# A CIN layer kernel: paired 64-row tiles for the Gram products, x1 stored with d innermost, and its sum over d moved to GpSimd

## The chip, the cores and the metric

The kernel runs on one core of a Trainium2 chip. The metric is the device time of one execution in microseconds. The profile's names for the engines are PE for TensorE (PEld for its weight loads), DVE for VectorE, ACT for ScalarE, POOL for GpSimd and SP for the engine that issues most DMAs.

## The reference, cut to what matters

Thirty-nine embedding tables are gathered into `e` of shape (512, 39, 16), a three layer CIN is applied with sums over `d` as its outputs, and a small MLP follows.

```python
def _cin_layer(X0, Xi, W, b):          # B, F0, D = 512, 39, 16; H = 128 outputs in each layer
    Wr = W.reshape(H, F0_, Fi)
    return jnp.einsum('hjk,bjd,bkd->bhd', Wr, X0, Xi) + b[None, :, None]
...
for W, b in Ws:                        # three layers
    Xi = _cin_layer(X0, Xi, W, b)
    res.append(Xi.sum(axis=2))         # the sum over d
z = jnp.concatenate(res, axis=1)
...
h = jnp.concatenate([z, dense_ctx], axis=1)
h = jnp.maximum(h @ W_top1 + b_top1, 0.0)
h = jnp.maximum(h @ W_top2 + b_top2, 0.0)
y = h @ W_top3
```

## The kernel before

The 512 samples are cut into 16 chunks of 32 samples, so a chunk has 32 x 16 = 512 columns (sample, d). A chunk is cut again into 4 groups of 8 samples, 128 columns (8 samples x 16 values of d), which are the 128 rows of a layer-1 product.

- **Layer 0** of the next chunk is built while the current one is in layer 1. GpSimd forms seven products `prod0` from shifted copies of x0 (`multiply0`), ScalarE rounds them to a high half (`round_product`), GpSimd subtracts for the low half (`split_product`), and TensorE adds three fp32r matmuls for each of the seven into the bank `acc0`. They stand behind the blocks of `L0_AFTER`, the last behind (3, 1), which means block 1 of group 3.
- **x1** is `acc0` plus a bias. ScalarE writes it to SBUF as `x1` (L759), copies that to the rounded `x1h` (L762), and VectorE writes the rest as `x1l` (L674).
- **Layer 1** of a group is 10 blocks of four fields each. A block is three matmuls of 512 columns (L528, L529, L530). Blocks marked A in `OWNERS = "ADADAADADA"` go to the PSUM banks `ya` and ScalarE scales them into `prods` (L779, four instructions a block, three in the last one); blocks marked D go to the banks `yd` and VectorE runs them into a chain (L651). There are 4 banks `ya` and 2 banks `yd`; a block waits with its first weight load (L528) until ScalarE or VectorE has emptied its bank. Two reductions of VectorE (L666) give `x2t`, which is x2 of the group with its 128 columns on the partitions.
- **Layer 2** only needs its sum over d, so a **Gram product** is formed for each group: `x2t` (128 rows of sample and d) times `diag`, a 128 x (8 x 40) matrix that holds the row's own x0 in the columns of its own sample. `gram_group` (L511) is one fp32 matmul of 320 columns over all 128 rows; the trace shows each as two weight loads and two matmuls. It stands behind block `G_AFTER = 6` of the following group. GpSimd writes `diag` (L401), in two buffers, and ScalarE empties the bank `misc` into `gram` (L767).
- **Layout.** Gathered embeddings are transposed by two matmuls into `misc` (`lay_out`, L479 and L480), go to SBUF as `xt`, from there to DRAM (`store_x0`, L319), and come back as `x0` (`load_x0`, L328) for a second turn (`turn_x0`), which is two transposes, of 117 rows (L487) and of 39 rows (L488), since x0 holds three shifted copies of 39 fields. They also come back as the tiles of layer 0 (L294, L288).
- **The sum of x1 over d** goes to `z`. For chunks 0 to 14 VectorE does it with one reduction inside the next group of blocks (`sum_dims` at (2, 0), L680); for the last chunk GpSimd does it in four additions that halve the number of values each time (`sum_dims_last`, L410 and L414).

Each engine runs a list written by hand; what binds them are semaphores. The loops over the middle chunks are real loops on VectorE and ScalarE and unrolled on TensorE, GpSimd and SP.

## Time and profile before

| what | us |
|---|---|
| median of 3 runs (lowest, highest) | 654.07 (651.15, 656.03) |
| the profiled execution, its own time | 654.38 |
| its span in the trace | 652.5 |
| busy: PE, DVE, ACT, POOL | 617.7, 581.6, 558.5, 470.9 |

The span runs from the first to the last instruction of the core, and the execution's own time is 1.9 us longer. The granted clock of TensorE was 1.0 in the whole span, the 2.4 GHz level. In the trace, first work takes about 38 us, then the chunks follow each other, and the last 50 us are the second layer's sum and the MLP.

### The profile page before, as it was taken

What the parts mean: (1) busy time and instruction counts of PE and PEld (TensorE: products, weight loads), DVE (VectorE), ACT (ScalarE), POOL (GpSimd) and SP (SyncE); (2) the same over time, 40 slices, a digit from 0 to 9 for tenths busy, and PEclk for the clock granted to TensorE, in tenths of its full rate; (3) what the DMA queues carried; (4) which work ended last, traced back from release to release, by engine and by line L of the source; (5) the groups of instructions that cost most, each with busy time, mean ns of one, the idle gap of its engine ahead of it and who ended that gap; (6) DMA issues with size and microseconds to landing.
All of it is one profiled execution on the core that took longest, in us unless ns stands there. A gap on an engine that the chain in (4) does not pass through costs nothing.

```text
span 652.5 us, 14351 instructions
## 1 busy us (share of the span) xinstructions
PE 617.7 (95%) x2595; PEld 477.3 (73%) x2595; DVE 581.6 (89%) x1233; ACT 558.5 (86%) x1767; POOL 470.9 (72%) x442
## 2 busy tenths in 40 slices
PE   0389999999999999999999999999999999999998
PEld 0146788787878787878788787878787878876673
DVE  0549999999999999999999999999999999999980
ACT  3048899999999999999899989999999999999782
POOL 6778898979797989989798979798987656420000
DMA  7533404131222314040414132231405050000200
GB/s 228 135 78 88 125 19 126 34 105 53 79 81 49 109 21 137 9 137 17 126 32 121 39 91 67 67 91 39 120 8 149 1 150 5 12 18 1 65 1 0
DMA packets 44274, 46.16 MB, mean 71 GB/s; under 512 B 20896, under 2 KB 27264, under 8 KB 44233
## 3 DMA queue, kind: packets, MB, share of 16 engines
...
HBM read 44.30 MB, written 1.31 MB: 70 GB/s over the span
## 4 chain that ended last, share of the span: by engine, by line
PE 88%; issue 4%; DVE 4%; POOL 1%; ACT 1%; DMA 1%; DVEq 0%
PE ya L528 12%; PE ya L530 12%; PE ya L529 12%; PE yd L528 9%; PE yd L530 8%; PE yd L529 8%; PE misc L511 5%; PE acc L500 4%; PE acc L499 3%; PE acc L501 3%; PE acc L504 2%; DVE chain L651 2%; POOL emb L390 1%; PE yd L611 1%; PE yd L609 1%
## 5 line engine op out<-in xcount | busy, mean ns | idle before, releaser
L779 ACT ACTIVATE prods<-ya,x0t 128x128 f32<-128x128 f32 x1472 | 452.0, 519 | 40.8 <-PE ya L530 37.8
L651 DVE SCALAR_TENSOR_TENSOR chain<-yd,x0t,chain 128x128 f32<-128x128 f32 x768 | 218.2, 343 | 4.9 <-remote 4.0
L390 POOL DMA_INDIRECT emb<-in_tables,rows x160 | 158.4, 990 | 35.4 <-issue 24.3
L528 PE MATMUL ya<-w1h,x1h 128*128 128x512 f32 (+1 forms) x384 | 166.4, 433 | 3.2 <-ACT prods L779 2.1
L437 POOL TENSOR_TENSOR prod0l<-prod,prod0h 120x512 fp32r<-120x512 f32 x98 | 127.6, 1302 | 47.8 <-ACT prod0h L788 47.2
L529 PE MATMUL ya<-w1l,x1h 128*128 128x512 f32 (+1 forms) x384 | 147.5, 384 | 0.0
L530 PE MATMUL ya<-w1h,x1l 128*128 128x512 f32 (+1 forms) x384 | 147.2, 383 | 0.0
L305 POOL TENSOR_TENSOR prod<-tiles,x0a 120x512 f32<-120x512 f32 x105 | 137.3, 1308 | 12.5 <-issue 4.2
L666 DVE TENSOR_REDUCE x2t<-prods 128x128 f32<-128x1792 f32 x64 | 129.2, 2019 | 2.4 <-issue 0.3
L666 DVE TENSOR_REDUCE prods<-prods 128x128 f32<-128x1536 f32 x64 | 111.7, 1746 | 0.1
L528 PE MATMUL yd<-w1h,x1h 128*128 128x512 f32 x256 | 102.5, 400 | 1.9 <-DVE prods L651 1.6
L530 PE MATMUL yd<-w1h,x1l 128*128 128x512 f32 x256 | 100.6, 393 | 0.0
L529 PE MATMUL yd<-w1l,x1h 128*128 128x512 f32 x256 | 100.2, 391 | 0.0
L528 PEld LDWEIGHTS ya<-w1h,x1h 128*128 128x128 f32 x384 | 72.2, 188 | 20.3 <-issue 4.3
L529 PEld LDWEIGHTS ya<-w1l,x1h 128*128 128x128 f32 x384 | 72.4, 189 | 15.5 <-issue 0.7
L530 PEld LDWEIGHTS ya<-w1h,x1l 128*128 128x128 f32 x384 | 72.0, 188 | 13.7
L788 ACT ACTIVATE prod0h<-prod 120x512 fp32r<-120x512 f32 x98 | 67.5, 689 | 1.1 <-POOL prod L305 1.1
L528 PEld LDWEIGHTS yd<-w1h,x1h 128*128 128x128 f32 x256 | 48.1, 188 | 20.5 <-DVE prods L651 8.2
L401 POOL TENSOR_TENSOR diag<-x0t,const 128x320 f32<-128x320 f32 x64 | 46.6, 728 | 17.0 <-PE misc L511 16.7
L529 PEld LDWEIGHTS yd<-w1l,x1h 128*128 128x128 f32 x256 | 48.0, 188 | 10.9 <-issue 0.5
L530 PEld LDWEIGHTS yd<-w1h,x1l 128*128 128x128 f32 x256 | 48.1, 188 | 10.3
L651 DVE SCALAR_TENSOR_TENSOR prods<-yd,x0t,chain 128x128 f32<-128x128 f32 x128 | 47.3, 464 | 0.0
...
## 6 DMA issues: line engine op xcount, KB each, us to landing
...
emb<-in_tables,rows POOLq DMA_INDIRECT x160
...
```

Of the source, the lines that this page charges most:

```text
L305: engine.tensor_tensor(prod0[:, i % L0_PRODS, :], tiles[:, slot, :], x0a[:, :], ALU.mult).then_inc(prod0_ready, 1)
L390: pool.indirect_dma_start(emb[:, c % 2, fo * D:(fo + 1) * D], None, a["tables"], bass.IndirectOffsetOnAxis(ap=rows[:, c, fo:fo + 1].bitcas ...
L401: pool.tensor_tensor(diag[:, n % 2, :, :], row.to_broadcast([P, GB, F1]), mask.to_broadcast([P, GB, F1]), ALU.mult).then_inc(diag_ready, 1)
L437: pool.tensor_tensor(prod0l[:, k % L0_PRODS, :], prod0[:, i % L0_PRODS, :], prod0h[:, k % L0_PRODS, :].bitcast(F32), ALU.subtract).then_in ...
L511: pe.matmul(misc[:, 0:GB * F1], x2t[:, g % 2, :], diag[:, g % 2, :, :].rearrange("p b j -> p (b j)"), start=True, stop=True).then_inc(g_do ...
L528: pe.matmul(out, x1h[:, c % 2, xs], w1h[:, cols], start=True, stop=False)
L529: pe.matmul(out, x1h[:, c % 2, xs], w1l[:, cols], start=False, stop=False)
L530: pe.matmul(out, x1l[:, c % 2, xs], w1h[:, cols], start=False, stop=True).then_inc(ready, 1)
L651: dve.scalar_tensor_tensor(out, product, x, run if step else b1[:, :], ALU.mult, ALU.add).then_inc(yd_used, 1)
L666: dve.tensor_reduce(out, src, AX.X, ALU.add).then_inc(sums_done, 1)
L779: mm = act.activation(prods[:, :, slot_of(q) + i], ya[(NA * g + k) % YA][:, i * H:(i + 1) * H], ACT.Copy, scale=turned(c)[:, g * F1 + j:g ...
L788: act.activation(prod0h[:, k % L0_PRODS, :], prod0[:, i % L0_PRODS, :], ACT.Copy).then_inc(prod0_high, 1)
```

## The change

Four things change together.

1. **The Gram product in row tiles.** The order of the columns of a chunk is changed so that partitions 0 to 63 of a group hold one half of its samples and 64 to 127 the other. A group's Gram product becomes two matmuls of 64 rows and 160 columns, one on the upper 64 rows, one on the lower, into two PSUM banks (`pair`). Two groups are done at one place (`gram_groups`, L527 of the new kernel): four matmuls behind (0, 6) and four behind (2, 6), none behind (1, 6) and (3, 6) except in the last chunk. `pair` takes a second bank, so `ya` has 3 banks in place of 4. `diag` is 160 columns wide, in four buffers.
2. **Layout.** x0 is stored in halves: 64-byte pieces where there were 128-byte ones on the way to DRAM, and rows of two 1 KB pieces on the way back. x0 holds two shifted copies, and its turn is two transposes of 78 rows.
3. **x1 with d innermost.** ScalarE writes `x1` from `acc0` in another order, and writes `x1h` from `acc0` too, no longer from `x1`, with no wait between them.
4. **The sum over d** of every chunk is done by GpSimd in place, in four additions, after its third product (after the sixth in chunk 0). VectorE's reduction is gone.

```diff
@@ -36,12 +36,15 @@
 CHUNKS = B // CB
 GB = P // D
 GROUPS = CB // GB
+HB = GB // 2
+HROWS = P // 2
...
 FT = P // D
-XB = 3
+XB = 2
...
-YA, YD = 4, 2
+YA, YD = 3, 2
+DIAGS = 4
...
-SUM_DIMS, SPLIT_X1 = (2, 0), (3, 0)
+SUM_AFTER, SUM_AFTER_0 = 2, 5
+SPLIT_X1 = (3, 0)
...
-        diag = sb("diag", [P, 2, GB, F1])
+        diag = sb("diag", [P, DIAGS, HB, F1])
...
-        scratch = nc.dram_tensor("x0_rows", (CHUNKS, FP, COLS), F32, kind="Internal").ap()
-
...
+        acc0, pair = ps("acc0"), ps("pair", (P, 2, 512))
+        misc = pair[:, 0, :]
...
         def chunk_rows(c):
-            return scratch[bass.ds(c, 1), :, :].rearrange("c r n -> (c r) n")
+            return scratch[bass.ds(c, 1), :, :, :].rearrange("c h r n -> r (c h) n")
+
+        def in_halves(x):
+            return x.rearrange("p (h n) -> p h n", h=2)
...
-                engine.dma_start(x0a[u * R0:(u + 1) * R0, :], chunk_rows(x)[0:R0, :]).then_inc(x0a_in, 16)
+                engine.dma_start(in_halves(x0a[u * R0:(u + 1) * R0, :]), chunk_rows(x)[0:R0]).then_inc(x0a_in, 16)
...
-                engine.dma_start(tiles[a:b, i % L0_TILES, :],
-                                 chunk_rows(x)[row:row + b - a, :]).then_inc(tile_in[i % L0_TILES], 16)
+                engine.dma_start(in_halves(tiles[a:b, i % L0_TILES, :]),
+                                 chunk_rows(x)[row:row + b - a]).then_inc(tile_in[i % L0_TILES], 16)
...
-                by_row = chunk_rows(x).rearrange("(f o) n -> f (o n)", f=FI)
-                for i, cols in enumerate((slice(0, FT * COLS), slice(FT * COLS, FO * COLS))):
-                    sp.dma_start(by_row[:, cols].rearrange("f (p b) -> p f b", b=CB),
-                                 xt[0:(cols.stop - cols.start) // CB, i, :].rearrange("p (f b) -> p f b", f=FI),
+                by_row = scratch[x, :, :, :].rearrange("h (f o) n -> (h f) (o n)", f=FI)
+                for i, cols in enumerate((slice(0, FT * HCOLS), slice(FT * HCOLS, FO * HCOLS))):
+                    sp.dma_start(by_row[:, cols].rearrange("q (p b) -> p q b", b=CB // 2),
+                                 xt[0:(cols.stop - cols.start) // (CB // 2), i, :].rearrange("p (q b) -> p q b", b=CB // 2),
...
-                    sp.dma_start(x0[g * F:(g + 1) * F, 0:COLS - g], chunk_rows(x)[0:F, g:COLS]).then_inc(x0_in, 16)
+                    sp.dma_start(in_halves(x0[g * F:(g + 1) * F, :])[:, :, 0:HCOLS - g], chunk_rows(x)[0:F, :, g:HCOLS]).then_inc(x0_in, 16)
...
             def block_diagonal(c, g):
                 n = GROUPS * c + g
                 pool.wait_ge(x0t_ready, c + 1)
-                wait_done(pool, g_done, n - 1)
+                wait_done(pool, g_done, n - DIAGS + 1)
                 row = x0t[:, c % XT, g * F1:(g + 1) * F1].rearrange("p (o j) -> p o j", o=1)
-                mask = const[:, C_MASK:C_MASK + GB].rearrange("p (b o) -> p b o", o=1)
-                pool.tensor_tensor(diag[:, n % 2, :, :], row.to_broadcast([P, GB, F1]),
-                                   mask.to_broadcast([P, GB, F1]), ALU.mult).then_inc(diag_ready, 1)
-
-            def sum_dims_last():
-
-                pool.wait_ge(x1h_ready, CHUNKS)
-                terms, count = x1[:, :].rearrange("p (g d b) -> p g d b", g=GROUPS, d=D), D
+                mask = const[:, C_MASK:C_MASK + HB].rearrange("p (b o) -> p b o", o=1)
+                pool.tensor_tensor(diag[:, n % DIAGS, :, :], row.to_broadcast([P, HB, F1]),
+                                   mask.to_broadcast([P, HB, F1]), ALU.mult).then_inc(diag_ready, 1)
+
+            def sum_dims(c):
+
+                pool.wait_ge(x1_ready, c + 1)
+                if c == 0:
+                    pool.wait_ge(l0_done, T0 + z_tiles)
+                terms, count = x1[:, :].rearrange("p (q d) -> p q d", d=D), D
                 while count > 2:
                     count //= 2
-                    pool.tensor_tensor(terms[:, :, 0:count, :], terms[:, :, 0:count, :], terms[:, :, count:2 * count, :],
+                    pool.tensor_tensor(terms[:, :, 0:count], terms[:, :, 0:count], terms[:, :, count:2 * count],
                                        ALU.add).then_inc(z_adds, 1)
-                    pool.wait_ge(z_adds, {8: 1, 4: 2, 2: 3}[count])
-                out = z[:, (CHUNKS - 1) * CB:].rearrange("p (g b) -> p g b", g=GROUPS)
-                pool.tensor_tensor(out, terms[:, :, 0, :], terms[:, :, 1, :], ALU.add).then_inc(z_sums, 1)
+                    pool.wait_ge(z_adds, 3 * c + {8: 1, 4: 2, 2: 3}[count])
+                out = z[:, c * CB:(c + 1) * CB].rearrange("p (g h b) -> p h b g", g=GROUPS, h=2)
+                one, other = (terms[:, :, d:d + 1].rearrange("p (h b g) d -> p h b (g d)", h=2, g=GROUPS) for d in range(2))
+                pool.tensor_tensor(out, one, other, ALU.add).then_inc(z_sums, 1)
...
-                    if c == CHUNKS - 1 and i == 2:
-                        sum_dims_last()
+                    if i == (SUM_AFTER if c else SUM_AFTER_0):
+                        sum_dims(c)
...
                 pe.transpose(misc[:, 0:XB * F], by_group[:, 0, :], const[0:XB * F, C_ID:C_ID + XB * F])
-                pe.transpose(misc[:, XB * F:GROUPS * F], by_group[0:F, XB, :], const[0:F, C_ID:C_ID + F]
+                pe.transpose(misc[:, XB * F:2 * XB * F], by_group[:, XB, :], const[0:XB * F, C_ID:C_ID + XB * F]
...
-            def gram_group(n, g):
-                pe.wait_ge(sums_done, 2 * n + 2)
-                pe.wait_ge(diag_ready, n + 1)
-                wait_done(pe, g_ready, n)
-                pe.matmul(misc[:, 0:GB * F1], x2t[:, g % 2, :],
-                          diag[:, g % 2, :, :].rearrange("p b j -> p (b j)"),
-                          start=True, stop=True).then_inc(g_done, 1)
+            def gram_groups(ns):
+
+                pe.wait_ge(sums_done, 2 * ns[-1] + 2)
+                pe.wait_ge(diag_ready, ns[-1] + 1)
+                wait_done(pe, g_ready, ns[0])
+                for i, n in enumerate(ns):
+                    for h in range(2):
+                        half, cols = slice(h * HROWS, (h + 1) * HROWS), slice(i * HB * F1, (i + 1) * HB * F1)
+                        mm = pe.matmul(pair[:, h, cols], x2t[half, n % 2, :],
+                                       diag[half, n % DIAGS, :, :].rearrange("p b j -> p (b j)"), start=True, stop=True)
+                mm.then_inc(g_done, len(ns))
...
-                            wait_done(pe, g_ready, GROUPS * c + g - 1)
+                            wait_done(pe, g_ready, GROUPS * c)
...
                             pe.wait_ge(x0_ready, c + 3)
-                            wait_done(pe, g_ready, GROUPS * c + g - 1)
+                            wait_done(pe, g_ready, GROUPS * c + 2)
                             turn_x0(c + 2)
-                        if q == G_AFTER and (g or prev):
-                            if not prev and g == 1:
-                                pe.wait_ge(x0t_ready, 2)
-                            if lay and g == lay_after(prev)[0]:
+                        if q == G_AFTER and g == 0 and prev:
+                            pe.wait_ge(x0t_ready, min(c + 2, CHUNKS))
+                            gram_groups((GROUPS * c - 2, GROUPS * c - 1))
+                        if q == G_AFTER and g == 2:
+                            if lay:
                                 pe.wait_ge(x0_ready, c + 3)
-                            if lay and g == turn_after(prev)[0]:
-                                pe.wait_ge(x0t_ready, c + 3)
-                            gram_group(GROUPS * c + g - 1, (g - 1) % GROUPS)
+                            gram_groups((GROUPS * c, GROUPS * c + 1))
+                        if q == G_AFTER and g == 3 and c == CHUNKS - 1:
+                            gram_groups((GROUPS * c + 2,))
...
-                                if nxt and (g, half) == SUM_DIMS:
-                                    sum_dims(c)
                                 if nxt and (g, half) == SPLIT_X1:
...
-                act.activation(xt[0:FO * D - P, 1, :], misc[0:FO * D - P, P:2 * P], ACT.Copy).then_inc(x0_ready, 1)
+                def by_half(x, order):
+                    return x.rearrange(f"p ({order} b) -> p f h b", h=2, b=CB // 2)
+
+                act.activation(by_half(xt[:, 0, :], "h f"), by_half(misc[:, 0:P], "f h"), ACT.Copy)
+                act.activation(by_half(xt[0:FO * D - P, 1, :], "h f"), by_half(misc[0:FO * D - P, P:2 * P], "f h"),
...
-                act.activation(x1[:, :].rearrange("p (g n) -> p g n", g=GROUPS),
-                               acc0[:, :].rearrange("p (n g) -> p g n", g=GROUPS), ACT.Identity, bias=bias[:, 0:1]).then_inc(x1_ready, 1)
-                act.wait_ge(x1_ready, c + 1)
-                act.activation(x1h[:, bass.ds(c & 1, 1), :].rearrange("p c n -> p (c n)"), x1[:, :],
-                               ACT.Copy).then_inc(x1h_ready, 1)
-
-            def evacuate_gram(n):
+                act.activation(x1[:, :].rearrange("p (h q d) -> p h d q", h=2, d=D),
+                               acc0[:, :].rearrange("p (h d q) -> p h d q", h=2, d=D), ACT.Identity, bias=bias[:, 0:1]).then_inc(x1_ready, 1)
+                act.activation(x1h[:, bass.ds(c & 1, 1), :].rearrange("p c (g n) -> p (c g) n", g=GROUPS),
+                               acc0[:, :].rearrange("p (n g) -> p g n", g=GROUPS), ACT.Identity, bias=bias[:, 0:1]).then_inc(x1h_ready, 1)
+
+            def evacuate_gram(n, i=0):
                 act.wait_ge(g_done, n + 1)
-                act.activation(gram[:, :, bass.ds(n * GB, GB)],
-                               misc[:, 0:GB * F1].rearrange("p (b j) -> p j b", b=GB),
+                cols = slice(i * HB * F1, (i + 1) * HB * F1)
+                act.activation(gram[:, :, bass.ds(n * GB, GB)].rearrange("p j (h b) -> p j h b", h=2),
+                               pair[:, :, cols].rearrange("p h (b j) -> p j h b", b=HB),
                                ACT.Copy).then_inc(g_ready, 1)
 
...
-                        if q == G_AFTER + 1 and (g or prev):
-                            evacuate_gram(GROUPS * c + g - 1)
+                        if q == G_AFTER + 1 and (g == 2 or g == 0 and prev):
+                            evacuate_gram(GROUPS * c + g - 2, 0)
+                        if q == G_AFTER + 2 and (g == 2 or g == 0 and prev):
+                            evacuate_gram(GROUPS * c + g - 1, 1)
+                        if q == G_AFTER + 1 and g == 3 and not nxt:
+                            evacuate_gram(GROUPS * c + 2)
```

TensorE around block (2, 6) of a middle chunk, before. `misc` is the bank of the Gram product.

```order
L529 MATMUL yd0<-w1l,x1h 128x512
L530 MATMUL yd0<-w1h,x1l 128x512
L511 MATMUL misc<-diag,x2t 128x320
L528 MATMUL ya0<-w1h,x1h 128x512
L529 MATMUL ya0<-w1l,x1h 128x512
```

The same place after; L544 to L546 are the three matmuls of a block there.

```order
L545 MATMUL yd0<-w1l,x1h 128x512
L546 MATMUL yd0<-w1h,x1l 128x512
L527 MATMUL pair<-diag,x2t 128x160 x4
L544 MATMUL ya1<-w1h,x1h 128x512
L545 MATMUL ya1<-w1l,x1h 128x512
```

One matmul of 320 columns has become four of 160, and the banks `ya` are taken in another turn.

TensorE around block (3, 6) before, with blocks 5, 6 and 7 of the group.

```order
L530 MATMUL ya1<-w1h,x1l 128x512
L528 MATMUL yd0<-w1h,x1h 128x512
L529 MATMUL yd0<-w1l,x1h 128x512
L530 MATMUL yd0<-w1h,x1l 128x512
L511 MATMUL misc<-diag,x2t 128x320
L528 MATMUL ya2<-w1h,x1h 128x512
```

Blocks 7, 8 and 9 of group 3 after, in the same stretch of the program.

```order
L544 MATMUL ya1<-w1h,x1h 128x512
L545 MATMUL ya1<-w1l,x1h 128x512
L546 MATMUL ya1<-w1h,x1l 128x512
L544 MATMUL yd1<-w1h,x1h 128x512
L545 MATMUL yd1<-w1l,x1h 128x512
L546 MATMUL yd1<-w1h,x1l 128x512
L544 MATMUL ya2<-w1h,x1h 128x384
L545 MATMUL ya2<-w1l,x1h 128x384
```

The Gram product is gone from here, so nothing but blocks stands between the turn of x0 behind (3, 1) and block (0, 3) of the next chunk.

GpSimd from the second product of a chunk to the fourth, before.

```order
L305 TENSOR_TENSOR prod0<-tiles,x0a 120x512
L437 TENSOR_TENSOR prod0l<-prod0,prod0h 120x512
L401 TENSOR_TENSOR diag<-x0t,const 128x320
L390 DMA emb<-in_tables,rows 128x16
L305 TENSOR_TENSOR prod0<-tiles,x0a 120x512
L437 TENSOR_TENSOR prod0l<-prod0,prod0h 120x512
L390 DMA emb<-in_tables,rows 128x16
L305 TENSOR_TENSOR prod0<-tiles,x0a 120x512
```

The same stretch after; `w0_z` is the tensor whose end holds `z`.

```order
L314 TENSOR_TENSOR prod0<-tiles,x0a 120x512
L449 TENSOR_TENSOR prod0l<-prod0,prod0h 120x512
L410 TENSOR_TENSOR diag<-x0t,const 128x160
L399 DMA emb<-in_tables,rows 128x16
L314 TENSOR_TENSOR prod0<-tiles,x0a 120x512
L449 TENSOR_TENSOR prod0l<-prod0,prod0h 120x512
L421 TENSOR_TENSOR x1<-x1 128x32x8
L421 TENSOR_TENSOR x1<-x1 128x32x4
L421 TENSOR_TENSOR x1<-x1 128x32x2
L426 TENSOR_TENSOR w0_z<-x1 128x8x4
L399 DMA emb<-in_tables,rows 128x16
L314 TENSOR_TENSOR prod0<-tiles,x0a 120x512
```

The four additions stand ahead of a gather and of the fourth product, and `diag` is half as wide.

## Rows read from the trace of the kernel before

**Rows 1.** The page: busy time of the engines, and the chain that ended last.

```profile
PE 617.7 (95%) x2595; PEld 477.3 (73%) x2595; DVE 581.6 (89%) x1233; ACT 558.5 (86%) x1767; POOL 470.9 (72%) x442
...
PE 88%; issue 4%; DVE 4%; POOL 1%; ACT 1%; DMA 1%; DVEq 0%
```

**Rows 2.** Busy time by stretch: chunk 9, then the last; length, busy of PE, PEld, DVE, ACT, POOL, clock.

```profile
365.20:400.30 35.10, 35.09 (x154) 28.09 (x154) 33.87 (x75) 32.58 (x110) 30.47 (x29) 1.00 0.28 74
540.70:576.00 35.30, 34.50 (x151) 27.67 (x151) 34.45 (x79) 32.80 (x107) 15.83 (x20) 1.00 0.05 14
```

**Rows 3.** Waits in 365.2 to 505.6, four chunks: total, times, longest, us.

```profile
POOL prod0l L437 <- ACT prod0h L788: 11.8, 11, 2.0
...
PEld yd L528 <- DVE prods L651: 1.2, 3, 0.4
```

**Rows 4.** TensorE in order of time at a Gram product: start, length in us.

```profile
373.74 0.70 PE L511 MATMUL misc<-diag,x2t 128*128 128x320 f32 x2
...
374.51 0.40 PE L529 MATMUL ya<-w1l,x1h 128*128 128x512 f32 x1
```

**Rows 5.** The same view where the layout is transposed, behind (2, 1).

```profile
378.28 0.27 PE L479 MATMUL misc<-const,emb 128*128 128x128 f32 x1
378.38 0.27 PE L480 MATMUL misc<-const,emb 128*32 128x128 f32 x1
...
378.73 0.39 PE L529 MATMUL ya<-w1l,x1h 128*128 128x512 f32 x1
```

**Rows 6.** The same view where x0 is turned, behind (3, 1).

```profile
387.88 0.26 PE L487 MATMUL misc<-const,x 117*128 117x117 f32 x1
388.07 0.19 PEld L488 LDWEIGHTS misc<-const,x 39*128 39x128 f32 x1 [0.22 <-issue]
...
388.31 0.19 PEld L528 LDWEIGHTS ya<-w1h,x1h 128*128 128x128 f32 x1
...
388.42 0.19 PEld L529 LDWEIGHTS ya<-w1l,x1h 128*128 128x128 f32 x1
...
388.88 0.39 PE L530 MATMUL ya<-w1h,x1l 128*128 128x512 f32 x1
```

**Rows 7.** ScalarE in order of time from x1 to block (3, 5).

```profile
388.08 0.69 ACT L759 ACTIVATE x<-acc,bias 128x512 f32<-128x512 f32 x1
388.96 0.63 ACT L762 ACTIVATE x1h<-x 128x512 f32 x1 [0.19 <-issue]
390.25 1.31 ACT L779 ACTIVATE prods<-ya,x0t 128x128 f32<-128x128 f32 x4 [0.66 <-PE ya L530]
...
393.17 1.33 ACT L779 ACTIVATE prods<-ya,x0t 128x128 f32<-128x128 f32 x4
```

**Rows 8.** Weight loads in order of time: of block (0, 0), and of (0, 3).

```profile
394.12 0.19 PEld L528 LDWEIGHTS ya<-w1h,x1h 128*128 128x128 f32 x1
...
396.54 0.19 PEld L528 LDWEIGHTS yd<-w1h,x1h 128*128 128x128 f32 x1 [0.43 <-DVE prods L651]
```

**Rows 9.** Groups by line, every shape apart: count, busy, mean ns.

```profile
L401 POOL TENSOR_TENSOR diag<-x0t,const 128x320 f32<-128x320 f32 x64 | 46.6, 728 | 17.0 <-PE misc L511 16.7
...
...
L680 DVE TENSOR_REDUCE w_z<-x 128x512 f32 x14 | 16.0, 1144 | 0.0
```

**Rows 10.** GpSimd in order of time: a late product at 321.64, the last chunk's additions.

```profile
321.64 1.28 POOL L305 TENSOR_TENSOR prod<-tiles,x0a 120x512 f32<-120x512 f32 x1 [1.75 <-issue]
...
568.16 1.69 POOL L410 TENSOR_TENSOR x<-x 128x256 f32<-128x256 f32 x3
569.92 0.25 POOL L414 TENSOR_TENSOR w_z<-x 128x32 f32<-128x32 f32 x1
```

**Rows 11.** SP's DMA issues in order of time: first layout, and chunk 9's.

```profile
18.56 0.93 SPq L319 DMA_DIRECT2D x_rows<-xt  x2
20.60 2.99 SPq L294 DMA_DIRECT2D tiles<-x_rows  x8
...
383.20 1.13 SPq L328 DMA_DIRECT2D x<-x_rows  x3
```

23 lines of the change are left out of this document (9 added, 14 removed).

## The prediction

> **What bounds the kernel now.** I read the page first. TensorE is busy in 95% of the span and holds 88% of the chain that ended last [rows 1]. A busy TensorE need not be the bound, so the next view is busy time by stretch. In a middle chunk of 35.1 us TensorE shows no idle time, VectorE has 33.87 of busy time, ScalarE 32.58, GpSimd 30.47, all at the full clock [rows 2]. The waits of four chunks show the slack: GpSimd waits 11.8 us for ScalarE, and TensorE's weight loads wait for VectorE only 1.2 [rows 3]. So the middle chunks go at TensorE's pace, with VectorE, ScalarE and GpSimd each 1 to 5 us behind the limit. In the last chunk, without layer 0, TensorE is no longer full and VectorE's 34.45 of 35.3 us decides [rows 2]. What a change on TensorE brings is therefore counted in chunks 1 to 14, by the starts of matmuls in order of time. Three matmuls of 512 columns start 0.23 us apart: the weights of the second go in at 388.42, when the first starts, and the third starts at 388.88 [rows 6].
>
> **The Gram products.** One takes 0.54 us: it starts at 373.74, L529 of the next block starts at 374.51, and the block's first matmul takes 0.23 of that [rows 4]. Four in a chunk are 2.16. After the change there are two places with four matmuls each, two of them on the upper 64 rows and two on the lower, each in two passes of 160 columns. A pass of 320 columns takes 0.27, one of 160 thus 0.134. Eight in a row are 1.07. The two passes of one matmul share rows and follow each other; a pass on other rows can lie beside the one ahead of it. With starts in order that leaves five pass lengths, 0.67. If every pass lies beside another it is 0.54.
>
> **Going into row tiles and out.** The trace has one matmul of at most 64 rows, the turn of 39 rows, and it is dear. Two transposes on all rows cost 0.22 (378.28 to the next block's first matmul, 378.73 less 0.23) [rows 5]; the turn's two, of 117 and 39 rows and fewer columns, cost 0.54 (387.88 to 388.42) [rows 6]. The cause can be seen: the weights of the 39-row one are not loaded ahead but at 388.07, 0.09 after the 117 columns have passed (by the 0.10 of 128 columns, 378.28 to 378.38 [rows 5]), and the next block's at 388.31, 0.10 after the 39 columns, and each load holds the matmul for 0.11 (388.31 to 388.42). Each crossing between the full array and 64 rows thus costs about 0.2, a visit 0.4. The Trainium skill, "TensorEngine Tiling (Array Packing)", section Key Properties, says that a change of tiling mode drains TensorE; by that rule this change pays at each of its two places a chunk, and the trace agrees. A place then costs 0.4 plus the body: 0.94, **1.07**, or 1.47 for bodies of 0.54, 0.67 and 1.07. There is a fourth value. If weight loads, 0.11 each, don't lie beside each other even on different rows, eight loads and the last pass give a body of 0.89 and a place of 1.29. No row shows two row tiles side by side, so the range is 0.94 to 1.47; I take 1.07, since loads and passes on other rows have no shared part that I can see in the trace. Two places are 2.14 against 2.16: **nothing gained** (bounds -0.28 and +0.78 a chunk).
>
> **The turn.** With 78 rows twice it never leaves the full array. By rows 5 it costs 0.22: **-0.3** a chunk (bounds -0.1 and -0.35).
>
> **The ring of three.** The load of block (0, 0) starts at 394.12 [rows 8]; with three banks it would have to wait until ScalarE has emptied block (3, 5), at 393.17 + 1.33 = 394.50 [rows 7]. The missing Gram product at (3, 6) and the cheaper turn bring TensorE there another 0.84 early, so 1.22 are missing. ScalarE comes earlier too. It starts `x1h` 0.88 after `x1`, with 0.19 of idle that goes with the removed wait, and it resumes blocks at 390.25 after 0.66 of idle [rows 7], although the matmul that it waited for, at 388.88 and 0.39 long, had ended by 389.27 [rows 6]. This late signal stands right behind the 39-row matmul. If both go, ScalarE is 0.85 early and TensorE stalls 0.4, of which a load that is ahead of its matmul hides 0.1: **+0.3** a chunk (bounds 0 and +1.0). At the other blocks of the chunk three banks are enough by the same comparison.
>
> **VectorE** loses its reduction of 1144 ns [rows 9]. It is not the bound; what it gives back is the wait at (0, 3), where the load sat idle 0.43 [rows 8], 1.2 us in four chunks, about half of it hidden by the load's lead: **-0.15** a chunk (bounds 0 and -0.3). ScalarE's Gram copies stay four of 320 elements, now two in a row twice a chunk. TensorE needs the bank again only at (2, 1) and (3, 1), four blocks or more later, so I cost that at nothing; without this cover it would be one copy.
>
> **GpSimd** gains four additions. Those of the last chunk took 2.01 us together (568.16 to 570.17) [rows 10]; now they read runs of 8, 4 and 2 values, not whole rows. It loses half of four `diag` of 728 ns [rows 9], at most 1.46 and at least 0. Net +0.9 (bounds +0.5 and, with additions at double time, +4.0). Behind them in its queue stand a gather, the fourth product and the second and third `prod0l`, for which TensorE waits at (1, 3) and (1, 8). The cover is its wait for ScalarE, 11.8/4 = 2.95 a chunk [rows 3], and the trace holds the experiment: at 321.64 a product came 1.75 late [rows 10], and the chunks kept their 35.1. So **0**, until the net addition passes about 2.9.
>
> **DMA.** The pieces to DRAM double, those of x0 and the tiles are twice as many at half the size, and one of three loads of x0 goes. In the middle x0 is issued by 384.33 (383.20 + 1.13) [rows 11] and used at 387.88, so nothing. In the beginning it is on the path: from the end of the issue of the first layout (18.56 + 0.93) to the first tile load at 20.60 are 1.11 us [rows 11]. Twice the pieces may double that: **+1.1** (bounds 0 and +2.5, with slower tile loads).
>
> **The sum.** A chunk: 0 - 0.3 + 0.3 - 0.15 = -0.15, in 14 chunks -2.1. Chunk 0 loses three Gram products and gains one place, 1.07 - 1.62 = -0.55, and its turn, -0.3. The beginning +1.1. The last chunk goes by VectorE and gains nothing. Together -1.85, so 654.4 becomes 652.5 in the profiled execution. The median of the three runs lies 0.3 below it, so I forecast **652**. Its own range, with the small bounds, is 648 to 656.
>
> **Rivals.**
> - *The array packs fully and the ring doesn't bind.* A place costs 0.94 and the stall is 0: per chunk -0.28 - 0.3 - 0.15 = -0.73, in 14 chunks -10.2, with the rest 644.5. For it: x1h and the turn may relieve ScalarE more than I count. Against it: two passes of a matmul share rows. The Trainium skill, "TensorE: Matmul & The Clock Gate", section Part 3, says that matmuls on different row tiles run beside each other, a few ns apart in their starts; no row here can show it.
> - *Weight loads don't overlap.* A place costs 1.29: +0.44 a chunk, +6.2 in all, 658.
> - *Row tiles run one after another* (the side of slower). A place costs 1.47: +0.8 a chunk, 11.2 in all, 663. It turns the change into a loss once a place costs over about 1.15.
> - *GpSimd becomes the bound.* If short runs make the additions twice as long, its busy time is 30.5 + 4.0 - 0.6 and its gaps between gathers come on top: some 0.5 a chunk more than TensorE needs, 660.
> - *The ring binds by its full 1.0 a chunk*, because ScalarE's late signal stays (it would now come behind each Gram place): +0.7 more, 662.
>
> **How the numbers follow.** Forecast 0.38, full packing 0.25, loads in a row 0.14, tiles in a row 0.10, GpSimd 0.04, ring 0.09. A measurement of this kernel tells about 1% (6.5 us) from nothing: faster is below 647.5, slower above 660.6. Faster has most of full packing and a little of the forecast, 0.28; slower has the tiles, the ring, half of GpSimd and a part of the loads, 0.24; the rest, 0.48, is within. The range reaches from full packing to between ring and tiles: 643 to 662.
>
> **What would show it.** Right: the weight load of the first L527 at a place starts only after the matmul ahead has passed, the place takes about 1.07 from its first matmul to the next block's, the turn about 0.22, the load of (0, 0) waits for ScalarE by some 0.3, no load waits for VectorE at (0, 3), GpSimd's additions take 2 us and its wait for ScalarE falls to about 2 a chunk, and the middle chunks take 34.9 to 35.0. Wrong: places of 0.9 or of 1.3 and more, a wait of TensorE for `prod0l`, waits for ScalarE in the other blocks of a chunk, or a first stage longer by over 2.5 us.

## The result

The changed kernel takes 659.1 us (median of 20 runs, 654.5 to 661.0), the kernel before 656.3 (20 runs, 651.2 to 658.1). The ratio is 1.0041 with an interval of 1.0028 to 1.0054: slower by 0.4%. The forecast was 652, a gain of 0.3%. The time is inside the range, the sign is wrong. The profiled execution took 659.05 us. Its span is 657.2 us, 4.7 more than the kernel before has: 1.6 of it lie ahead of the third turn, 0.6 between the third and the fourth, and 2.6 in the twelve chunks behind that, while the end is 0.2 shorter.

The page of the changed kernel, busy time and chain, beside [rows 1]:

```profile
PE 611.0 (93%) x2723; PEld 469.2 (71%) x2723; DVE 568.9 (87%) x1218; ACT 568.4 (86%) x1767; POOL 476.8 (73%) x502
...
PE 75%; ACT 7%; issue 6%; DVE 3%; POOL 3%; DMA 3%; ACTq 2%; another core or an unknown queue 1%; SPq 1%; DVEq 0%; POOLq 0%
```

TensorE has 6.7 us less to do and the span is longer. Its share of the last chain fell from 88 to 75%. Busy time by stretch, a middle chunk, beside [rows 2] (length, then busy of PE, PEld, DVE, ACT, POOL, clock):

```profile
356.21:391.50 35.29, 34.57 (x164) 27.52 (x163) 33.10 (x74) 33.38 (x109) 31.02 (x32) 1.00 0.28 71
```

A middle chunk takes 35.29 in place of 35.12, though TensorE is busy in only 34.57 of it. TensorE in order of time at a Gram place, beside [rows 4], and at the turn, beside [rows 6]:

```profile
368.13 0.40 PE L546 MATMUL yd<-w1h,x1l 128*128 128x512 f32 x1
368.46 0.57 PEld L527 LDWEIGHTS pair<-diag,x2t 64*128 64x128 f32 x8 [0.37 <-issue]
368.46 0.81 PE L527 MATMUL pair<-diag,x2t 64*128 64x160 f32 x8
...
369.54 0.40 PE L545 MATMUL ya<-w1l,x1h 128*128 128x512 f32 x1
...
391.42 0.23 PE L499 MATMUL pair<-const,x 78*128 78x78 f32 x1
391.49 0.28 PE L500 MATMUL pair<-const,x 78*128 78x78 f32 x1
...
391.88 0.39 PE L545 MATMUL ya<-w1l,x1h 128*128 128x512 f32 x1
```

The matmul ahead of the place ends at 368.13 + 0.23 = 368.36, the next block's first one starts at 369.54 - 0.23 = 369.31: the place takes 0.95, the price of full packing (0.94). The turn takes 391.88 - 0.23 - 391.42 = 0.23. Both parts are as cheap as the more hopeful figures had them. So the question is where the gain went.

ScalarE at the same end of a chunk, beside [rows 7], then the weight loads and starts of (0, 0) and (0, 3), beside [rows 8]:

```profile
391.82 1.16 ACT L771 ACTIVATE x<-acc,bias 128x512 f32<-128x512 f32 x1
392.77 0.65 ACT L773 ACTIVATE x1h<-acc,bias 128x512 f32 x1
393.53 1.30 ACT L791 ACTIVATE prods<-ya,x0t 128x128 f32<-128x128 f32 x4
```

```profile
397.89 0.47 PE L544 MATMUL ya<-w1h,x1h 128*128 128x512 f32 x1 [0.76 <-ACT prods L791]
...
400.06 0.50 PE L544 MATMUL yd<-w1h,x1h 128*128 128x512 f32 x1
```

The write of x1 with d innermost takes 1.16 us where it took 0.69, and TensorE now stands idle 0.76 at (0, 0). Counted from the start of the turn to the block's first matmul, (0, 0) is reached at 397.89 - 391.42 = 6.47; before, at 394.30 - 387.88 = 6.42. And (0, 3) is reached at 400.06 - 391.42 = 8.64; before, at 396.55 - 387.88 = 8.67. These blocks didn't move, whatever was taken off TensorE ahead of them. The two matmuls before:

```profile
394.30 0.40 PE L528 MATMUL ya<-w1h,x1h 128*128 128x512 f32 x1
...
396.55 0.50 PE L528 MATMUL yd<-w1h,x1h 128*128 128x512 f32 x1
```

VectorE in order of time from the end of (3, 1) shows why, first in the changed kernel, then in the kernel before:

```profile
391.12 0.35 DVE L668 SCALAR_TENSOR_TENSOR chain<-yd,x0t,b 128x128 f32<-128x128 f32 x1 [1.00 <-issue]
...
392.31 2.02 DVE L683 TENSOR_REDUCE x2t<-prods 128x128 f32<-128x1792 f32 x1
394.25 1.12 DVE L668 SCALAR_TENSOR_TENSOR chain<-yd,x0t,chain 128x128 f32<-128x128 f32 x4
395.38 0.75 DVE L691 SCALAR_TENSOR_TENSOR x1l<-acc,bias,x1h 128x512 f32 x1
396.05 1.12 DVE L668 SCALAR_TENSOR_TENSOR chain<-yd,x0t,chain 128x128 f32<-128x128 f32 x4
397.08 1.75 DVE L683 TENSOR_REDUCE prods<-prods 128x128 f32<-128x1536 f32 x1
...
399.25 0.75 DVE L668 SCALAR_TENSOR_TENSOR prods<-yd,x0t,chain 128x128 f32<-128x128 f32 x2
```

```profile
387.61 0.35 DVE L651 SCALAR_TENSOR_TENSOR chain<-yd,x0t,b 128x128 f32<-128x128 f32 x1
...
395.76 0.73 DVE L651 SCALAR_TENSOR_TENSOR prods<-yd,x0t,chain 128x128 f32<-128x128 f32 x2
```

In the changed kernel VectorE has stood idle 1.00 and starts on (3, 1) when TensorE has finished it; in the kernel before it comes straight from the block ahead, and starts at the same place all the same, 0.27 ahead of the turn in place of 0.30. From there it works without a gap until (3, 8) is done: 399.25 + 0.75 - 391.12 = 8.88 us, before 395.76 + 0.73 - 387.61 = 8.88. There are two `yd` banks, and (0, 3) needs the one that (3, 8) leaves. So a chunk has **two parts**: from (3, 1) to (0, 3) VectorE sets the time, from (0, 3) to (3, 1) TensorE does. The change took the Gram product at (3, 6) and 0.3 of turn out of the first part, where TensorE now waits instead, and in the second part it put two pairs (2 x 0.95) in place of three single products (3 x 0.54): 1.90 for 1.62. Counted from block to block, a single one costs 0.57 to 0.62 there, so the pairs cost 0.14 more, and that is the difference of part 2 in e4 below (26.59 to 26.45). The other 0.06 of the changed kernel's +0.20 come with GpSimd's additions, which e4 doesn't have in these chunks.

### The profile page after: what moved, and what is told of

The parts are those of the page before. It is cut to its first block, busy times and chain, and to the rows that moved or that the text cites. A ratio compares the mean times of both kernels' runs of the same rounds, so it can differ in the third digit from the quotient of the medians.

```text
span 657.2 us, 14603 instructions
## 1 busy us (share of the span) xinstructions
PE 611.0 (93%) x2723; PEld 469.2 (71%) x2723; DVE 568.9 (87%) x1218; ACT 568.4 (86%) x1767; POOL 476.8 (73%) x502
## 2 busy tenths in 40 slices
DMA packets 70291, 44.90 MB, mean 68 GB/s; under 512 B 30928, under 2 KB 69264, under 8 KB 70249
## 4 chain that ended last, share of the span: by engine, by line
PE 75%; ACT 7%; issue 6%; DVE 3%; POOL 3%; DMA 3%; ACTq 2%; another core or an unknown queue 1%; SPq 1%; DVEq 0%; POOLq 0%
PE ya L544 11%; PE ya L546 11%; PE ya L545 10%; PE yd L544 7%; PE yd L546 7%; PE yd L545 7%; ACT prods L791 6%; PE pair L527 3%; PE acc L512 3%; PE acc L511 3%; PE acc L513 3%; PE acc L516 2%; POOL emb L399 2%; DVE chain L668 2%; PE yd L628 1%
## 5 line engine op out<-in xcount | busy, mean ns | idle before, releaser
L544 PE MATMUL ya<-w1h,x1h 128*128 128x512 f32 (+1 forms) x384 | 156.7, 408 | 13.9 <-ACT prods L791 10.7
L546 PE MATMUL ya<-w1h,x1l 128*128 128x512 f32 (+1 forms) x384 | 147.2, 383 | 0.0
L544 PE MATMUL yd<-w1h,x1h 128*128 128x512 f32 x256 | 103.5, 404 | 2.9 <-DVE prods L668 1.5
L546 PE MATMUL yd<-w1h,x1l 128*128 128x512 f32 x256 | 100.5, 393 | 0.0
L544 PEld LDWEIGHTS ya<-w1h,x1h 128*128 128x128 f32 x384 | 73.0, 190 | 37.3 <-issue 24.8
L546 PEld LDWEIGHTS ya<-w1h,x1l 128*128 128x128 f32 x384 | 72.3, 188 | 13.8
L544 PEld LDWEIGHTS yd<-w1h,x1h 128*128 128x128 f32 x256 | 48.1, 188 | 21.8 <-DVE prods L668 5.7
L546 PEld LDWEIGHTS yd<-w1h,x1l 128*128 128x128 f32 x256 | 48.2, 188 | 10.8
L668 DVE SCALAR_TENSOR_TENSOR chain<-yd,x0t,b 128x128 f32<-128x128 f32 x64 | 22.5, 351 | 30.0 <-PE yd L546 15.1
```

The lines of the kernel that those rows point to most:

```text
L544: pe.matmul(out, x1h[:, c % 2, xs], w1h[:, cols], start=True, stop=False)
L546: pe.matmul(out, x1l[:, c % 2, xs], w1h[:, cols], start=False, stop=True).then_inc(ready, 1)
L668: dve.scalar_tensor_tensor(out, product, x, run if step else b1[:, :], ALU.mult, ALU.add).then_inc(yd_used, 1)
```

## The experiments

The runs came in five sets, each set on one chip beside the kernel before. In the table, worked out from the starts of TensorE's instructions in each trace, "chunk" is the median time from turn to turn in chunks 4 to 14, "part 1" the time from the first transpose of a turn to the weight load of (0, 3), "part 2" the rest, in us; the ratio is the measured one to the kernel before on the same chip. The changed kernel itself ran in the first comparison and in the second set alone.

```
run                      chunk  part 1  part 2  ratio (95%)
before                   35.12   8.67    26.45
changed                  35.29   8.64    26.65   1.0041 (1.0028-1.0054)
e8_after_again           35.27   8.63    26.64   1.0039 (1.0020-1.0057)
e1_ring3                 35.13   8.68    26.45   1.0008 (0.9999-1.0017)
e2_x1_flat               35.24   8.61    26.63   1.0068 (1.0054-1.0081)
e3_x1_late               35.26   8.61    26.65   1.0060 (1.0044-1.0075)
e4_sum_dve               35.14   8.55    26.59   1.0024 (1.0013-1.0035)
e10_sum_alone            35.10   8.63    26.47   1.0031 (1.0021-1.0042)
e7_sum_at_g3             35.68   9.10    26.58   1.0109 (1.0081-1.0138)
e14_one_reduce_late      34.77   7.60    27.17   0.9987 (0.9974-1.0000)
e16_one_late_sum_dve     34.68   7.60    27.08   0.9938 (0.9923-0.9953)
e5_pairs_odd             34.98   8.87    26.11   0.9974 (0.9955-0.9992)
e6_pairs_odd_late        35.04   8.90    26.14   0.9997 (0.9975-1.0019)
e11_pairs_odd_sum_dve    34.84   8.74    26.10   0.9962 (0.9948-0.9976)
e12_lay_early            34.83   8.96    25.87   0.9951 (0.9936-0.9966)
e13_reduces_late         35.15   8.38    26.77   1.0023 (1.0013-1.0033)
e15_pairs_odd_one_late   35.13   8.38    26.75   0.9998 (0.9988-1.0008)
```

### First set: the ring and ScalarE

My first theory was the ring: TensorE waits at (0, 0) for ScalarE. **e1_ring3** is the kernel before with three of its four `ya` banks in use.

```diff
-                    out, ready = ya[(NA * g + k) % YA], ya_ready
-                    wait_done(pe, ya_used, NA * n + k - YA + 1)
+                    out, ready = ya[(NA * g + k) % RING_A], ya_ready
+                    wait_done(pe, ya_used, NA * n + k - RING_A + 1)
```

> The kernel before, with ScalarE's blocks of layer 1 going round three PSUM banks in place of four; nothing else is changed. Theory A (the ring): in the changed kernel TensorE's first block of each chunk waits about 1.1 us more than before for ScalarE to give a bank back, and in the stall near 43 us it has one block less to run on. Here ScalarE is later still than in the changed kernel at the end of a chunk (the wait and the copy of x1 are before's), so this should cost 0.5 to 1.5 us a chunk, 7 to 20 us in all, and show as idle time of TensorE put down to ScalarE. Rival B (GpSimd's additions and its waits make the changed kernel late): the ring costs nothing, the time stays within 1 us of the kernel before. Rival C (only the start is lost): 2 to 4 us, all of it before the chunk that ends near 110 us, and the period of 35.12 us a chunk stays.

Measured 650.3 against 649.7. Three banks alone cost nothing that a chunk shows (35.13): the kernel before gets to (0, 0) late enough. That contradicts the 0.5 to 1.5 a chunk of theory A.

**e2_x1_flat** and **e3_x1_late** are the changed kernel with less of ScalarE's work ahead of (0, 0).

```diff
-                act.activation(x1[:, :].rearrange("p (h q d) -> p h d q", h=2, d=D),
-                               acc0[:, :].rearrange("p (h d q) -> p h d q", h=2, d=D), ...
+                act.activation(x1[:, :], acc0[:, :], ...)                # e2
...
+                        if nxt and (g, q) == (3, 7):                     # e3: x1 behind x1h and block (3, 7)
+                            evacuate_x1_late(c + 1)
```

> The changed kernel, with x1 written in the order in which it lies in PSUM, so without the turn that puts d innermost, and GpSimd's four additions over d as contiguous blocks. Theory A (the ring of three, and ScalarE's late end of a chunk): the write of x1 falls from 1.16 us to about 0.69, ScalarE is 0.47 us earlier at block (0,0), and TensorE, which waits for it there, gains the same 0.47 a chunk, about 6.6 us over 14 chunks: some 652.5 against 659 of the changed kernel, and below the kernel before. Rival B (GpSimd): the additions are no shorter, no gain beyond 1 us. Rival C (the start alone): no gain beyond 1 us in the chunks of the middle, period stays 35.3.

> The changed kernel, with ScalarE's write of x1 (still 1.16 us, d innermost) moved from in front of the rounded copy to behind block (3,7) of the same chunk; VectorE's split and the first blocks of the next chunk then wait only for the rounded copy. Theory A: what sets the first block of the next chunk is the whole of ScalarE's work from (3,1) to (3,5), 1.16 us of it the write, so TensorE's wait of about 1.1 us at (0,0) goes and part of it (0.2 to 0.5) may come back at (0,2): a gain of 0.6 to 1.1 us a chunk, 8 to 15 us in all. Rival B (GpSimd late): no gain, or a loss, since GpSimd's first addition gets x1 later. If the ring only passes the lateness on (ScalarE has no slack in a whole chunk), the gain is below 0.2 a chunk.

Both contradict the ring theory: the chunk is 0.05 and 0.03 shorter than the changed kernel's, not 0.47 and 0.6 to 1.1. By line, e2's write of x1 is down to 0.69 us, and e3's load of (0, 3), turn at 387.58, is shown second:

```profile
L771 ACT ACTIVATE x<-acc,bias 128x512 f32<-128x512 f32 x15 | 10.4, 691 | 0.5 <-PE acc L516 0.5
```

```profile
396.19 0.19 PEld L544 LDWEIGHTS yd<-w1h,x1h 128*128 128x128 f32 x1 [1.05 <-DVE prods L668]
```

TensorE does pass (0, 0) earlier, its first matmul at 5.7 behind the turn in place of 6.47. Then it waits at (0, 3) for VectorE, and gets there at 8.61, as in the changed kernel. Taking off a wait moved it three blocks on.

**e4_sum_dve** puts the sum over d back on VectorE, in group 2, with the rest of the change left in.

```diff
-                    if i == (SUM_AFTER if c else SUM_AFTER_0):           # GpSimd
+                    if c == CHUNKS - 1 and i == SUM_AFTER:
...
+                                if nxt and (g, half) == (2, 0):          # VectorE: one reduction of 16 neighbours
+                                    sum_dims(c)
```

> The changed kernel, with the sum over d back on VectorE as one reduction of 16 neighbours at the place that it had before (group 2 of the chunk); GpSimd's four additions remain in the last chunk alone. ScalarE, the ring, the pairs of row tiles stay. Theory A: VectorE (568.9 us busy of 657) has room for 1.1 us a chunk, GpSimd's additions cost nobody anything: within 1.5 us of the changed kernel, either way. Rival B (GpSimd's 2 us of additions make its products, and with them ScalarE's roundings and TensorE's layer 0, late): a gain of 0.2 to 0.5 a chunk, 3 to 7 us. Rival D (VectorE binds behind the ring): a loss of 0.15 a chunk or more, 2 us and up.

It has the ratio 1.0024, e2 and e3 on the same chip 1.0068 and 1.0060: GpSimd's additions cost 2.6 to 3.1 us. Against e3 about half of it is 0.12 a chunk (35.26 to 35.14), and the other half comes once. In e3's first chunk the product of GpSimd that follows the additions starts at 73.03, in e4 at 70.44, and ScalarE waits for it (waits of e3, 68 to 77 us):

```profile
ACT prod0h L803 <- POOL prod L314: 1.6, 1, 1.6
```

That chunk, third turn to fourth, takes 36.3 in e3 and 34.9 in e4.

### Second set: where the time is set

**e8_after_again** is the changed kernel itself.

> The changed kernel itself, unchanged, beside the other runs of this set, so that they can be compared on one chip. Each theory: ratio to the kernel before as measured (1.004, 1.0028 to 1.0054). What the start shows is of interest: if the standstill of ScalarE, VectorE and TensorE near 43 to 47 us is missing here as it was in the four runs before, the loss has to come from the chunks in the middle (0.17 a chunk, 2.2 us) and from the first chunk, not from that standstill.

The ratio repeats. On this chip, as in the first comparison (but in no kept trace of the other sets), ScalarE and VectorE stand still for some 4 us between 40 and 47, in all six kept traces. Busy time by stretch there, changed kernel, then before:

```profile
46.00:52.00 6.00, 4.60 (x14) 3.58 (x15) 4.82 (x13) 4.56 (x18) 4.36 (x5) 0.72 0.47 135
```

```profile
46.00:52.00 6.00, 3.33 (x14) 2.28 (x15) 4.45 (x12) 4.64 (x19) 4.24 (x4) 1.00 0.44 123
```

In the changed kernel the granted clock of these 6 us is 0.72, so part of it runs at 1.2 GHz and not at 2.4, after TensorE had stood idle from about 44; in the kept trace of the kernel before it stayed at 1.00. In e8 it is 0.50. The third turn comes at 73.5 in the changed kernel and at 71.9 before. The cause of the standstill stays open. The lower clock is not the changed kernel's alone: on this chip 23 of 27 executions of the kernel before have a mean clock below 1.0 too, 8 of 10 of the changed kernel. Among executions with the same mean clock the changed kernel is slower by as much (658.4 against 655.2 at 0.997, 659.8 against 656.9 at 0.995), so the clock doesn't explain the ratio.

**e5_pairs_odd** moves the pairs from groups 0 and 2 to 1 and 3, so that each part has one, and ScalarE's copies of the second pair into the next chunk; **e6_pairs_odd_late** adds e2's and e3's edits.

```diff
-                        if q == G_AFTER and g == 0 and prev:
-                            gram_groups((GROUPS * c - 2, GROUPS * c - 1))
-                        if q == G_AFTER and g == 2:
-                            gram_groups((GROUPS * c, GROUPS * c + 1))
+                        if q == G_AFTER and g == 1:
+                            gram_groups((GROUPS * c - 1, GROUPS * c) if prev else (0,))
+                        if q == G_AFTER and g == 3:
+                            gram_groups((GROUPS * c + 1, GROUPS * c + 2))
```

> The changed kernel, with the two places of paired Gram products moved from groups 0 and 2 to groups 1 and 3 (still behind block 6), and ScalarE's copies of the second pair moved into the next chunk, behind blocks (0,4) and (0,6). Theory V, formed after the first four runs: a chunk has two parts. From (3,1) to (0,3) VectorE sets the time: it runs 8.9 us without a gap from the end of block (3,1) to the end of block (3,8), and block (0,3) needs its bank, 8.6 us behind the turn in every kernel so far. From (0,3) to (3,1) TensorE sets it: 26.45 us with three single Gram products, 26.64 with two pairs. The change took its work out of the part that VectorE sets. With one pair in each part the second falls to 25.7 us and the first holds at 8.6: 34.35 a chunk against 35.29, some 12 us less than the changed kernel in all (range 8 to 13), 9 less than the kernel before. Rival A (the ring and ScalarE set the first part): the pair at (3,6) comes on top of TensorE's wait at (0,0), no gain, or at most 0.3 a chunk. Rival B (GpSimd): no gain.

> As the run with the pairs at groups 1 and 3, and besides x1 written in the order of PSUM, behind block (3,7). Theory V: ScalarE's earlier end lets TensorE pass (0,0) as soon as it comes, but (0,3) waits for VectorE as before, so within 1.5 us of the run without it. Rival A: another 0.5 to 1 us a chunk, 7 us and more.

The sign is right and the size is not: 34.98, not 34.35. Part 2 fell by 0.5, part 1 rose by 0.2, because VectorE's bound doesn't end at (0, 3). The loads of e5 (turn at 388.58) wait there, right until VectorE has done (3, 8) at 396.66 + 0.72 = 397.38, and again at (0, 8):

```profile
396.66 0.72 DVE L666 SCALAR_TENSOR_TENSOR prods<-yd,x0t,chain 128x128 f32<-128x128 f32 x2
```

```profile
397.43 0.19 PEld L544 LDWEIGHTS yd<-w1h,x1h 128*128 128x128 f32 x1 [0.53 <-issue]
```

```profile
402.02 0.19 PEld L544 LDWEIGHTS yd<-w1h,x1h 128*128 128x128 f32 x1 [0.60 <-DVE chain L666]
```

I had taken the end of VectorE's stretch for fixed; with less slack in TensorE's part it reaches further. e6 gains nothing over e5 (656.2 against 654.2; theory V had them within 1.5 of each other), so rival A's further gain isn't there.

**e7_sum_at_g3** is e4 with x1 late and VectorE's reduction over d inside the stretch, beside the split of x1.

```diff
-SUM_DIMS = (2, 0)
+SUM_DIMS = (3, 0)
```

> The changed kernel, with ScalarE's write of x1 behind block (3,7) and the sum over d on VectorE as one reduction (about 1.1 us), but placed behind its block (3,3), next to the split of x1, and not in group 2 as in the earlier run. Theory V: the reduction now lies in the unbroken stretch of VectorE that ends with block (3,8) and frees the bank for (0,3), so the whole of it shows: 1.0 to 1.15 us a chunk more than the run with the sum in group 2 (651.2), 12 to 16 us in all. Rival A (ScalarE and the ring) and rival T (VectorE has room over the whole chunk, 34 of 35.1 us busy): within 2 us of that run.

The reduction takes less than I thought, since its 16 terms are neighbours now (1144 ns before [rows 9]):

```profile
L698 DVE TENSOR_REDUCE w_z<-x 128x512 f32 x14 | 9.5, 678 | 0.0
```

Part 1 grew by 0.55, the chunk by 0.54. In group 2 the same instruction costs next to nothing: e16 below, which has it there and no additions on GpSimd, is even 0.09 a chunk shorter than e14. The total of VectorE is equal in e7 and e4: its place decides. That e7 also writes x1 late is not the cause, since e3 does so with part 1 at 8.61.

### Third set: the halves of the change, and putting it right

**e10_sum_alone** is the kernel before with GpSimd's sum and x1 with d innermost only.

> The second half of the change alone, on the kernel before: x1 written with d innermost, the rounded copy taken from PSUM without a wait, and GpSimd's four additions in every chunk in place of VectorE's reduction; the Gram products, the turn, the four banks for ScalarE's blocks and the order of rows in DRAM stay as before. Theory V: VectorE's reduction lay in group 2, where TensorE sets the time, so taking it away gives nothing; GpSimd's additions cost 0.05 to 0.12 us a chunk (as between the two earlier runs of which one had the sum on GpSimd, 35.26 a chunk, the other on VectorE, 35.14) and 1.3 us once in the first chunk: 2 to 3 us slower than the kernel before. Rival W (VectorE, 33.9 of 35.1 us busy, sets the pace of the whole chunk): 0.3 to 0.8 us a chunk faster, 4 to 11 us in all.

Measured +2.5 us (652.2 against 649.6), as theory V said. Most chunks take about 35.1, but three of them 35.3 to 36.1, and the chunk from the third turn to the fourth takes 35.9 in place of 34.7. In the worst a load of `x0a`, which layer 0 reads, came late by 1.60, and GpSimd, busier by its additions, had not made it up 15 us later; TensorE waits for its product (GpSimd's late product of e10, then a weight load near 334):

```profile
318.90 1.28 POOL L305 TENSOR_TENSOR prod<-tiles,x0a 120x512 f32<-120x512 f32 x1 [1.60 <-DMA x0a<-x_rows]
```

```profile
333.95 0.19 PEld L502 LDWEIGHTS acc<-prod0h,w0h 120*128 120x128 f32 x1 [0.97 <-POOL prod0l L440]
```

In the kernel before a product that was 1.75 late [rows 10] cost nothing. But late chunks are not tied to the additions alone: e16, without them, has one of 35.5, in which a product of GpSimd came 2.1 late.

**e11_pairs_odd_sum_dve** joins e5 and e4's edit. **e12_lay_early** moves the layout transposes from (2, 1) to (0, 7) besides.

> The kernel with the pairs at groups 1 and 3, with the sum over d back on VectorE in group 2, as one reduction of 16 neighbours (0.68 us). Theory V: GpSimd's cost goes (1.3 us once and about 0.1 a chunk); VectorE's 0.6 comes back in group 2, where VectorE waits 0.9 us for TensorE, so mostly hidden: 1.5 to 3 us less than the run with the sum on GpSimd, a ratio to the kernel before of 0.993 to 0.996. Rival W (VectorE sets the whole chunk by now): 0.3 to 0.6 us a chunk more, no gain or a loss of up to 5 us.

> As the run before it, with the two layout transposes (0.33 us of TensorE a chunk) moved from behind block (2,1), in the part that TensorE sets, to behind block (0,7), where TensorE waits 0.6 us for VectorE's bank at (0,8); ScalarE's copies of the late Gram pair go behind (0,2) and (0,4) for it. Theory V: 0.2 to 0.33 us a chunk less, 3 to 4.5 us, unless VectorE is full by then (33.6 us busy of 34.9). Rival W: no gain.

e11 (0.9962) lies at the edge of what theory V had, 0.993 to 0.996, and has none of rival W's loss. e12's chunk stays (34.83): part 2 fell by 0.23 and part 1 grew by 0.22, so rival W held there; the 0.6 us between its median and e11's are within the intervals of both.

### Fourth and fifth set: VectorE's order

**e14_one_reduce_late** is e3 with one reduction of VectorE (1.75 us, the first half of group 3) behind its block (3, 8) and not ahead of it. **e13_reduces_late** does this in e11, and moves a second reduction behind (0, 3).

```diff
                         for q in own:
                             multiply_add(c, g, q)
+                            late = (g, half) == (3, 1)                   # e13: in ((3, 1), (0, 0))
+                            if late and q == own[0]:
+                                continue
                             if q != own[0]:
...
-                                continue
+                                if not late:
+                                    continue
```

> The changed kernel with x1 written behind block (3,7), as in the earlier run of that name (35.26 a chunk, block (0,3) 8.61 behind the turn, TensorE's load waiting 1.05 there), and one of VectorE's reductions (1.75 us, the first half of group 3) moved from between its blocks (3,6) and (3,8) to behind (3,8). VectorE does the same work in another order. Theory V: the bank for (0,3) comes back 1.75 earlier, so (0,3) is reached at 7.6 to 8.0 in place of 8.61; VectorE is as late as before from its block (0,1) on, and takes back a part at (0,8), where it has to finish (0,3): 34.6 to 35.0 a chunk, 3 to 9 us less than the earlier run. Rival W (VectorE's total sets the pace, whatever its order): 35.2 a chunk, no change beyond 1 us. Rival A (ScalarE and the ring): no change at (0,3).

> The best version so far but one (pairs at groups 1 and 3, the sum over d on VectorE in group 2; 34.84 a chunk, ratio 0.9962), with two of VectorE's reductions moved behind the block that they stood ahead of: the first half of group 3 behind (3,8), the second half of group 3 behind (0,3) of the next chunk. Theory V: the waits of TensorE at (0,3) (0.15 or so) and at (0,8) (0.6) go, what is left is VectorE's total and ScalarE, which needs the slots of the second reduction at (0,5) and may wait 0.5 there: 34.3 to 34.6 a chunk, 3 to 7 us less, a ratio to the kernel before of 0.986 to 0.992. Rival W: no change beyond 1 us.

e14 shows it. VectorE in order of time has (3, 8) done at 390.54 + 0.76 and the reduction behind it; the load of (0, 3) at 391.88 waits for nothing, 7.61 behind the turn (384.27) in place of 8.61:

```profile
390.54 0.76 DVE L668 SCALAR_TENSOR_TENSOR prods<-yd,x0t,chain 128x128 f32<-128x128 f32 x2
391.12 1.72 DVE L683 TENSOR_REDUCE prods<-prods 128x128 f32<-128x1536 f32 x1
```

```profile
391.88 0.19 PEld L544 LDWEIGHTS yd<-w1h,x1h 128*128 128x128 f32 x1
```

The same work in another order: 35.26 became 34.77 a chunk, the ratio 1.0060 became 0.9987. Half of the 1.01 comes back between (0, 4) and (0, 7), where ScalarE now waits 0.46 for the slots that the reduction reads and a load of TensorE 0.48 for ScalarE:

```profile
394.39 0.19 PEld L544 LDWEIGHTS ya<-w1h,x1h 128*128 128x128 f32 x1 [0.48 <-ACT prods L798]
```

e13 is a miss: 1.0023, not 0.986 to 0.992. The longer chunk doesn't come from the second move: **e15_pairs_odd_one_late**, with the first alone, has it too (35.13, where e11 has 34.84). Its ratio is lower than e13's, 0.9998; what the second move costs outside of the median chunk stays open. But **e16_one_late_sum_dve**, e14 with the sum on VectorE, has both gains.

> The kernel with the one reduction behind (3,8) (34.77 a chunk, ratio 0.9987), with the sum over d on VectorE in group 2 in place of GpSimd's additions. If the causes add up: 1.3 to 1.5 us less in the chunk behind the first, no single late chunk (0.7), 0 to 0.1 a chunk: 2 to 3.5 us less, a ratio of 0.993 to 0.996. If VectorE's 0.68 us more in group 2 now shows, since it has less slack at 34.8 a chunk: no gain.

> The kernel with the pairs at groups 1 and 3 and the sum over d on VectorE (34.84 a chunk, ratio 0.9962), with only the first of the two reductions moved, behind (3,8). If the causes add up: the wait at (0,3) goes (0.36), that at (0,8) stays, ScalarE waits up to 0.5 at (0,4): 34.5 to 34.8 a chunk, 0.5 to 4 us less, a ratio of 0.990 to 0.995. If (0,8) is what holds this version, and VectorE is no earlier there: no change.

e15's forecast, 34.5 to 34.8, is missed as well. ScalarE in order of time, e14, then e15 with VectorE ahead of it:

```profile
393.04 1.31 ACT L798 ACTIVATE prods<-ya,x0t 128x128 f32<-128x128 f32 x4 [0.46 <-DVE prods L683]
```

```profile
390.68 0.61 DVE L666 SCALAR_TENSOR_TENSOR chain<-yd,x0t,chain 128x128 f32<-128x128 f32 x2 [0.50 <-PE yd L546]
...
393.75 1.30 ACT L803 ACTIVATE prods<-ya,x0t 128x128 f32<-128x128 f32 x4 [1.58 <-DVE prods L681]
```

In e15 the Gram pair at (3, 6) brings (3, 8) later, VectorE waits 0.5 for it, and the reduction behind it comes so late that ScalarE stands 1.58. The two cures share one slack and don't add up. e16 has the lowest ratio of all: 646.1 against 650.1 of the kernel before on its chip, 0.9938, though its interval overlaps those of e11 and e12. It is faster than the kernel before, and by its ratio than the changed one, beside which it did not run.

## Why the prediction was wrong

- **"So the middle chunks go at TensorE's pace"** is the step that failed. It was read from TensorE's busy time in a whole chunk, 35.09 of 35.10 [rows 2]. The rows had the sign: the load of (0, 3) sat idle 0.43 for VectorE [rows 8]. I priced it as a small wait that VectorE's lost reduction would remove. But that reduction lay in group 2, and in the stretch ahead of (0, 3) VectorE does 8.88 us in both kernels. What was gained on TensorE there, 0.54 + 0.31, turned into waits, at (0, 0) and (0, 3). Shown by e2, e3 and e7, and by e14.
- **The Gram places.** The place is 0.95, the first rival's 0.94, not 1.07: passes on other rows do run beside each other. The sum compared four products with two places, 2.16 with 2.14. Where TensorE sets the time it is three with two: 1.62 with 1.90. By block starts that is +0.14, as e4 has it (26.59 to 26.45); with GpSimd's additions it is the +0.2 of the changed kernel (26.65).
- **The turn**: 0.23 as costed, but of the 0.3 gained nothing reached the end.
- **The ring of three**, +0.3: TensorE is idle 0.76 at (0, 0). Counted from x1, ScalarE's start of blocks came 0.46 earlier (1.71 to the next block in place of 2.17), not 0.85: I left the write with d innermost at its old 0.69, and it takes 1.16. Counted from the turn it came only 0.26 earlier (2.11 in place of 2.37), since x1 itself starts 0.20 later behind the turn; that the two Gram copies in a row ahead of it do this, which I had put at nothing, is argued from the order of ScalarE's work. Still it costs little by itself, as (0, 3) comes at 8.6 anyway (e2, e3).
- **VectorE**, -0.15: 0 in fact, the reduction stood where VectorE had slack (in e10, without it, the chunk is 35.10 in place of 35.12).
- **GpSimd**, 0: the additions took 1.64 + 0.25 as costed, and still cost some 2.5 us: in e10 1.2 once in the first chunk and the rest in single late chunks, in e3 against e4 1.4 once and 0.12 a chunk. The mean slack of 2.95 a chunk says nothing of the chunk in which a transfer is late.
- **DMA**, +1.1: not settled. Between the two traces the first turn is no later (32.7 to 33.1 before), and the 1.6 at the third turn come with the standstill near 45 and TensorE's clock; what causes them was not tested. On the chips without the standstill the second turn comes at 44.2 and 43.7 in the two kernels with the old layout (e1, e10) and at 44.6 to 45.9 in the nine with the new one, so some 1 us may well be right; these are single traces of kernels that differ in other things too.

So a middle chunk was forecast at -0.15 and measured at +0.17. In e4, with the sum on VectorE, it is +0.02 (part 1 -0.12, part 2 +0.14): the gains that the sum took from the turn and from VectorE didn't arrive. The other 0.15 came with GpSimd's additions. In e10, on the kernel before, the same additions lengthen no median chunk; why they do beside the rest of the change stays open.

Right were the price of the turn, that row tiles aren't serial, and "nothing gained" by the two row tile places, though for another reason.
